# A language-model tower on one core: token gathers issued later in the front loop, factors one by one, beta by pairs behind the loop, and a re-ordered start of the attention loop

## The chip, the core and the metric

The kernel runs on one core of one Trainium2 chip. The metric is the device time of one execution in microseconds (us), the median of several runs. The core's engines work from queues of their own and meet at semaphores: TensorE (PE in the profile, its weight loads PEld), VectorE (DVE), ScalarE (ACT), GpSimd (POOL), and SyncE (SP), which here only issues DMAs.

## What is computed

Inputs are two rows of 1024 token ids. Three blocks follow one another, each added to the stream `h` of 2 x 1024 x 192 values:

```
tok = wte[ids];  Q = layernorm(tok)*gamma + beta, times W_proj.T;  V = tok @ W_val.T          (8 heads of 64)
traces = 0.99*(value_traces - erase(Q masked)/denom) + 0.1*(Q_masked^T V two tokens on)/denom
h  = (Q one token back @ traces) @ W_out.T
h += attention(layernorm(h)): softmax(q k^T * scale * (gw gw^T)), mixed with gw gw^T by sigmoid(alpha)
     gw = softmax(gelu(v @ W_gp))                                                  (49 groups)
h += soft mixture of 64 experts (layernorm(h)), dispatch and combine by softmax of x @ phi_n
```

`denom` is the count of masked tokens times 8, at least 1.

## The kernel before, in words

Tokens are worked in NT = 16 tiles of 128 (8 for each of the two rows of the batch, KT = 8). The order of every engine is written out by hand, as one program for each engine with waits on counting semaphores; an engine runs its program strictly in this order.

*Front loop.* The rows of `wte` come by NX = 18 indirect DMAs (`gather(g)`, L463), nine for each batch row, so that tile i of the first row is token block i, but tile i of the second row is block i + 1 (`tok_of`, L375: tile 8 is block 9, tile 15 is block 16). POOL issues them. Its program in the loop over i is: gather(i + 6), then `masked(i)` (L477, a masked copy of the normalised tile), then, for odd i, `front_factors(i + 2, i + 4)` (L471 and L472), which takes the statistics of two tiles and makes 1/sqrt(var) and -mean/sqrt(var). For these factors it waits until VectorE has done `stats` (L1534 to L1537) of both tiles, and `stats(i)` waits for block `tok_of(i)` to land.

Stage s of the front loop, on the other engines:
- ScalarE: the hi part of tile s - 2 (L1165), normalise tile s (L1157, waits for the factors), squares and masked copy of Q of tile s - 3 (L1172, L1177).
- TensorE: Q projection of tile s - 3 (`q_proj`, L597 to L601, waits for the lo part), two transposes of tile s - 1 (`tok_T`), two products with the next token block (`cprime(s - 2)`, L670 and L671, waits for `masked`), 16 small products (`grams(s - 5)`, L692).
- VectorE: the lo part of tile s - 2 (`lo_parts`, L1562 and L1563), norms and scaled Q of tile s - 4 (L1577 to L1587), then the statistics that `ahead(s)` lists: tiles 3 and 4 in stage 2, 5 in stage 3, 6 and 7 in stage 4, and tile s + 3 from stage 5 on.
- SyncE: weights of later stages, each load released by a count of `stats`: wT at 6, wvT and vt at 8, wpn at 10, woT, wpg and aw at 12.

Ahead of the loop TensorE makes the row beta x W_proj (L637, L638), the count of masked tokens (L642), and beta x W_proj once more with tokens' channels on the partitions (L645, L646), which VectorE copies to `bpair` (L1551).

*Behind the loop* the traces are mixed with W_out and the attention's q x k matrix is prepared in parts (`prepare`, SETUP); each part is rounded up on ScalarE and its remainder taken on VectorE (`round_off`, L1505; for the parts "B2" a further instruction, L1518, rewrites one row). Part "kB2" ends with the copy of `bpair` to `wpn`.

*Second loop* (16 tiles): mix, normalise, transpose, value projection (`value_proj`), and in its last four stages `query(0)` to `query(3)`; queries 4 and 5 and the transposes `gw_T(0)`, `gw_T(1)` of the group weights follow.

*Attention loop.* Stage s on TensorE: `scores(s)` (10 products into banks 0 and 1, 4 into banks 2 and 3), `turn(s - 1)` (8 transposes, L889), `attend(s - 1)` (L900, L901, 16 products L907). In stage 1, between scores and turn, stand `sums(0)` (L831), `gw_T(2)`, `gw_T(3)` and `sums(1)`, all waiting until VectorE has taken all eight queries; `turn(0)` then waits for both `u_take`. VectorE's stage: weight, copy of half of `et` (L1768), `z_tile(s)` (L1759), `finish(s - 1)`, and then `beside(s)`: the square sums of phi in stage 3 (L1733), its scaling in halves in stages 4 and 5 (L1739), the lo part of its first half in stage 7 (L1749) and of the rest in stage 8 (L1751). Dispatch, experts and combination follow.

## Time and profile before

| | us |
|---|---|
| median of 3 runs (463.87 to 464.69) | 464.32 |
| the profiled execution | 464.32 |
| its span in the trace | 462.5 |
| TensorE busy | 431.2 (93%) |
| VectorE busy | 297.3 (64%) |
| ScalarE busy | 228.5 (49%) |
| GpSimd busy | 145.4 (31%) |
| chain that ended last, TensorE's share | 69% |

```profile
PE   5889998999888999999999989999999889999995
DVE  6489873586765577676777676766965243443564
ACT  4577742588743446554232566877874312122220
POOL 5778600375010065120003490003540331212310
```

Each digit is the busy share, in tenths, of a slice of 11.6 us. The front loop fills slices 1 to 6, the second loop slices 8 to 10, the attention loop begins in slice 11. A row of a timeline reads: start, duration, engine, line, operation, output <- inputs, their sizes, and in brackets the engine's idle time just before and what ended it. A duration runs from an instruction's start to its end and can overlap its neighbours'; the distance of two starts is what an instruction costs its engine.

### The profile page before, as it was taken

What the parts mean: (1) busy time and instruction counts of PE and PEld (TensorE: products, weight loads), DVE (VectorE), ACT (ScalarE), POOL (GpSimd) and SP (SyncE); (2) the same over time, 40 slices, a digit from 0 to 9 for tenths busy, and PEclk for the clock granted to TensorE, in tenths of its full rate; (3) what the DMA queues carried; (4) which work ended last, traced back from release to release, by engine and by line L of the source; (5) the groups of instructions that cost most, each with busy time, mean ns of one, the idle gap of its engine ahead of it and who ended that gap; (6) DMA issues with size and microseconds to landing.
All of it is one profiled execution on the core that took longest, in us unless ns stands there. A gap on an engine that the chain in (4) does not pass through costs nothing.

```text
span 462.5 us, 8303 instructions
## 1 busy us (share of the span) xinstructions
PE 431.2 (93%) x3086; PEld 356.7 (77%) x3086; DVE 297.3 (64%) x776; ACT 228.5 (49%) x415; POOL 145.4 (31%) x235
## 2 busy tenths in 40 slices
PE   5889998999888999999999989999999889999995
PEld 2667755798777888988888878899975577787895
DVE  6489873586765577676777676766965243443564
ACT  4577742588743446554232566877874312122220
POOL 5778600375010065120003490003540331212310
PEclk9999999999999999999999999999999999999999
DMA  3343000200100000500000000003629999999404
GB/s 97 111 126 104 11 2 0 103 1 1 30 0 0 1 0 1 206 1 0 1 0 1 1 1 0 2 0 132 280 100 412 388 351 380 382 373 386 152 19 136
DMA packets 14231, 49.64 MB, mean 107 GB/s; under 512 B 3504, under 2 KB 8528, under 8 KB 9968
## 3 DMA queue, kind: packets, MB, share of 16 engines
q1 hardware_dynamic: 7584, 43.21, 24.8%
q0 software_dynamic: 2912, 3.37, 2.6%
q10 hardware_dynamic: 3696, 2.54, 1.8%
q8 instruction: 25, 0.41, 0.4%
q14 instruction: 14, 0.11, 0.1%
HBM read 45.94 MB, written 3.15 MB: 106 GB/s over the span
## 4 chain that ended last, share of the span: by engine, by line
PE 69%; DMA 12%; DVE 11%; POOL 3%; issue 2%; ACT 2%; SPq 0%; POOLq 0%; ACTq 0%; DVEq 0%
DMA w1r<-in_p_w 10%; PE ps L907 9%; PE ps L953 8%; PE ps L1110 6%; PE ps L1051 3%; PE ps L889 3%; PE ps L1080 2%; PE ps L933 2%; DMA tok<-in_L_tok_wte,ints 2%; PE ps L937 2%; PE ps L936 2%; PE ps L934 2%; PE ps L935 2%; PE ps L1097 2%; PE ps L854 1%
## 5 line engine op out<-in xcount | busy, mean ns | idle before, releaser
L907 PE MATMUL ps<-pr,et 128*128 128x192 f32 x256 | 46.6, 333 | 2.1 <-DVE et L1768 1.6
L1110 PE MATMUL ps<-ys,ct 128*128 128x192 f32 x256 | 45.2, 331 | 1.7 <-DMA ys<-ys_dram 1.7
L1937 DVE TENSOR_TENSOR res<-ps,res 128x384 f32<-128x384 f32 x64 | 35.7, 558 | 15.2 <-PE ps L1110 10.7
L907 PEld LDWEIGHTS ps<-pr,et 128*128 128x128 f32 x256 | 41.1, 189 | 5.4 <-ACT et L1332 3.1
L1110 PEld LDWEIGHTS ps<-ys,ct 128*128 128x128 f32 x256 | 41.2, 190 | 5.1 <-issue 4.8
L501 POOL TENSOR_SCALAR ve<-mv 128x1 f32<-128x1 f32 x32 | 12.1, 378 | 94.8 <-DVE mv L1783 54.0
L585 POOL DMA_DIRECT2D ys<-ys_dram x32 | 19.6, 617 | 69.8 <-DMA ys_dram<-ysb 68.7
L1451 ACT ACTIVATE hs<-ps 128x384 f32<-128x384 f32 x16 | 7.8, 490 | 58.5 <-PE ps L1051 58.5
L1321 ACT ACTIVATE scs<-ps,pr 128x1024 f32<-128x1024 f32 x16 | 17.8, 1115 | 29.2 <-PE ps L858 29.2
L1325 ACT ACTIVATE zz<-zz,nmx 128x1024 f32<-128x1024 f32 x16 | 18.4, 1150 | 27.7 <-DVE nmx L1762 27.4
L1928 DVE COPY ysb<-ps 128x192 f32<-128x192 f32 x16 | 5.7, 356 | 39.0 <-PE ps L1080 39.0
L1798 DVE CUSTOM_DVE_ANT_0 ec<-ps,zero 128x1024 f32<-128x1024 f32 x16 | 19.5, 1222 | 13.8 <-PE ps L937 13.8
L1051 PE MATMUL ps<-w1r,xsT 128*32 128x384 f32 x256 | 24.0, 492 | 1.7 <-DMA w1r<-in_p_w 1.6
L1457 ACT COPY ct<-ps 128x1024 f32<-128x1024 f32 x16 | 16.1, 1009 | 14.8 <-PE ps L1097 14.8
L953 PE MATMUL ps<-x2a,lsr 128*128 128x193 f32 x128 | 22.6, 327 | 0.0
L953 PE MATMUL ps<-x2b,lsr 128*128 128x193 f32 x128 | 21.7, 328 | 0.7 <-ACT lsr L1363 0.7
L502 POOL TENSOR_TENSOR rstd<-ve,mhalf 128x1 f32<-128x1 f32 x32 | 21.3, 667 | 2.7
L1768 DVE COPY et<-ps 128x512 f32<-128x512 f32 x16 | 11.1, 692 | 16.6 <-PE ps L889 16.5
L953 PEld LDWEIGHTS ps<-x2b,lsr 128*128 128x128 f32 x128 | 20.9, 190 | 1.0 <-ACT lsr L1363 1.0
L538 POOL TENSOR_TENSOR xve<-xve,mhalf 128x2 f32<-128x2 f32 x8 | 7.4, 921 | 45.2 <-DVE xve L1869 45.2
L953 PEld LDWEIGHTS ps<-x2a,lsr 128*128 128x128 f32 x128 | 20.8, 190 | 0.2
L463 POOL DMA_INDIRECT tok<-in_L_tok_wte,ints x18 | 18.5, 1025 | 7.8 <-issue 5.1
(318 smaller groups left out, 1197.6 us busy)
## 6 DMA issues: line engine op xcount, KB each, us to landing
w1r<-in_p_w SPq DMA_DIRECT2D x16, 1152.0 KB, 19.4
w2r<-in_p_w SPq DMA_DIRECT2D x16, 1152.0 KB, 19.2
ys_dram<-ysb ACTq DMA_DIRECT2D x16, 96.0 KB, 8.3
ys<-ys_dram POOLq DMA_DIRECT2D x32, 48.0 KB, 7.2
phT<-in_p_phi SPq DMA_DIRECT2D x1, 1024.0 KB, 4.6
wT<-in_p_qkv SPq DMA_DIRECT2D x1, 774.0 KB, 4.2
out<-res SPq DMA_DIRECT2D x3, 192.0 KB, 3.3
out<-res ACTq DMA_DIRECT2D x3, 192.0 KB, 3.8
```

Source lines behind the costliest of these rows:

```text
L463: nc.gpsimd.indirect_dma_start(tok[:, g, :], None, a["L0_tok_wte"], bass.IndirectOffsetOnAxis(ap=ints[:, g:g + 1], axis=0)).then_inc(gathe ...
L502: return nc.gpsimd.tensor_tensor(rstd[:, i:i + 1], ve[:, i:i + 1], mhalf[:, 0:1], ALU.pow)
L585: nc.gpsimd.dma_start(ys[rows, t % YR, b, :], y4[b]).then_inc(ys_loaded[t % YR], 16)
L907: last = mm(d[:, 0:D], et[:, k, :], pr[:, b * KT + k, 1:1 + D], start=(k == 0), stop=(k == KT - 1))
L953: last = mm(d, ls(b, k)[:, t * P:(t + 1) * P], x2(i)[:, 0:1 + D], start=(k == 0 and t % 2 == 0), stop=(k == KT - 1), skip_group_check=True)
L1051: last = mm(bank(0)[32 * j:32 * j + 32, 0:HID], xsT[:, half, GE * g + j, :, :].rearrange("d b s -> d (b s)"), w1r[r][:, 3 * (j // 2) + j % ...
L1110: last = mm(bank(5 + q % 3)[:, h * D:(h + 1) * D], ct[:, u % 2, k + h, :], ys[:, t % YR, b, :], start=True, stop=True)
L1321: sc.activation(scs[:], bank(0, 2), ACT.Identity, bias=pr[:, i, 0:1]).then_inc(m["s_copied"], 1)
L1325: sc.activation(zz[:, i % 2, :], zz[:, i % 2, :], ACT.Exp, bias=nmx[:, i:i + 1], accum_out=rsum[:, i:i + 1]).then_inc(m["e_ready"], 1)
L1457: sc.copy(ct[:, u % 2].rearrange("p k c -> p (k c)"), bank(3, 2)).then_inc(m["cT_copied"], 1)
L1798: v.tensor_tensor_reduce(ec(i), bank(logit_bank(i), 2), bc(zero[:], [P, NS]), 1.0, LOWEST, ALU.add, ALU.max, mxC[:, i:i + 1]).then_inc(m[" ...
L1937: v.tensor_tensor(res[:, i:i + 2, :], bank(5 + q % 3)[:, 0:2 * D].rearrange("p (h d) -> p h d", h=2), res[:, i:i + 2, :], ALU.add).then_in ...
```

## The change

- POOL: factors of tiles 1 and 2 are made one by one, tile 1's ahead of gather 3; gathers 5 and 6 no longer stand behind `masked(0)`; in the loop gather(i + 4) takes the place of gather(i + 6).
- VectorE: the statistics of tiles 1 and 2 stand ahead of the wait for beta; `ahead` becomes tiles 3 and 4 in stage 2, then 5, 6, 7 in stages 3 to 5, 8 and 9 in stage 6, tile s + 3 from stage 7 on. The count of masked tokens is taken in stage 2.
- TensorE: nine products of a tile of ones ahead of the wait for inputs; `cprime` one stage later; the products L645 and L646 go. In their place four products of one row with ones stand ahead of part "kB2", and `bpair` goes. L1518 goes from all "B2" parts.
- Second loop: only queries 0 and 1 stand in it; ScalarE takes them one stage earlier.
- Attention loop: `sums(0)` in stage 1 and `sums(1)` in stage 2, each waiting only for what it needs, `gw_T(2)` and `gw_T(3)` at the ends of stages 2 and 3, with their takes on ScalarE and VectorE; `z_tile(1)` ahead of `u_take(0)`; `norm_groups(1)` moves from stage 0 to the end of stage 1. Square sums of phi in stage 5, both halves of its scaling in stage 6, both lo parts in stage 8.

```diff
@@ POOL
+            front_factors(1, 2)
             gather(3)
+            front_factors(2, 3)
             gather(4)
-            front_factors(1, 3)
             pool.wait_ge(m["mask_ready"], 1)
             masked(0)
-            gather(5)
-            gather(6)
             for i in range(1, NT):
-                if i + 6 < NX:
-                    gather(i + 6)
+                if i + 4 < NX:
+                    gather(i + 4)
                 masked(i)
                 if i % 2 and i + 2 < NT:
                     front_factors(i + 2, min(i + 4, NT))
@@ PE
+            pe.wait_ge(m["ones_ready"], 1)
+            for k in range(9):
+                mm(bank(2)[:, 0:P], ones[:], ones[:], start=True, stop=True)
...
-            mm(bank(3)[:, 0:1], ones[:], msum[:], start=True, stop=True)
-            for t in range(HP):
-                c, o = slice(t * P, (t + 1) * P), slice(2 + 2 * t, 4 + 2 * t)
-                mm(bank(3)[:, o], wpT[:, 0, c], betA, start=True, stop=False)
-                last = mm(bank(3)[:, o], wpT[0:DB, 1, c], betB, start=False, stop=True)
-            last.then_inc(m["cnt_filled"], 1)
+            mm(bank(6)[:, 0:1], ones[:], msum[:], start=True, stop=True).then_inc(m["cnt_filled"], 1)
...
-                if 2 <= s < NT + 2:
-                    cprime(s - 2)
+                if 3 <= s < NT + 2:
+                    cprime(s - 3)
+                if s == NT + 1:
+                    cprime(NT - 1)
...
+            for t in range(HP):
+                mm(setup_bank("kB2")[:, 272 + 2 * t:274 + 2 * t], wpT[DB:DB + 1, 1, t * P:(t + 1) * P],
+                   ones[DB:DB + 1, 0:2], start=True, stop=True)
             prepare("kB2", at["kA"] + 1)
...
-                if s > NT:
+                if NT < s <= NT + 2:
                     query(s - NT - 1)
...
             def sums(b):
 
-                pe.wait_ge(m["qpl_taken"], 2 * QPS)
+                pe.wait_ge(m["gw_ready"], b + 1)
+                pe.wait_ge(m["qpl_taken"], 2 * QPS - 2 + b)
...
-                if s == 1:
-                    sums(0)
-                    for j in range(GTS, NB * GTS):
-                        gw_T(j)
-                    sums(1)
+                if 1 <= s <= NB:
+                    sums(s - 1)
                 if s >= 1:
                     turn(s - 1)
...
+                if 2 <= s < 2 + GTS:
+                    gw_T(s)
@@ DVE
-                    link(remainder(B2[DB:DB + 2, :], d[DB:DB + 2, 0:n], scale[2], B2[DB:DB + 2, :]))
-                    last = v.tensor_scalar(B2[DB:DB + 1, :], d[DB:DB + 1, 0:n], scale[3], None, ALU.mult)
+                    last = remainder(B2[DB:DB + 1, :], d[DB:DB + 1, 0:n], scale[2], B2[DB:DB + 1, :])
...
-                if s <= 4:
-                    return {2: [3, 4], 3: [5], 4: [6, 7]}.get(s, [])
+                if s <= 6:
+                    return {2: [3, 4], 3: [5], 4: [6], 5: [7], 6: [8, 9]}.get(s, [])
                 return [s + 3] if s + 3 < NT else []
...
             for s in range(NT + 1):
                 if s == 1:
-                    u_take(0)
-                    for j in range(GTS, NB * GTS):
-                        gw_lo(j)
-                    u_take(1)
+                    z_tile(1)
+                if 3 <= s < 3 + GTS:
+                    gw_lo(s - 1)
+                if 1 <= s <= NB:
+                    u_take(s - 1)
```

## Rows read from the trace of the kernel before

**Rows 1.** The page, busy time by engine: share of span, instructions
```profile
PE 431.2 (93%) x3086; PEld 356.7 (77%) x3086; DVE 297.3 (64%) x776; ACT 228.5 (49%) x415; POOL 145.4 (31%) x235
```

**Rows 2.** DVE timeline, front loop: start, us, line, form, idle before
```profile
31.30 0.36 DVE L1534 BATCH_NORM_STATS2 st<-tok 128x6 f32<-128x192 f32 x1 [0.58 <-DMA tok<-in_L_tok_wte,ints]
...
32.05 0.28 DVE L1562 TENSOR_TENSOR XL<-ps,XH 128x128 fp32r<-128x128 f32 x1
...
35.11 0.28 DVE L1562 TENSOR_TENSOR XL<-ps,XH 128x128 fp32r<-128x128 f32 x1
...
37.26 0.35 DVE L1534 BATCH_NORM_STATS2 st<-tok 128x6 f32<-128x192 f32 x1
...
49.82 0.28 DVE L1562 TENSOR_TENSOR XL<-ps,XH 128x128 fp32r<-128x128 f32 x1
```

**Rows 3.** POOL timeline, front loop
```profile
8.57 0.28 POOL L472 TENSOR_TENSOR nmr<-nmean,rstd 128x1 f32<-128x1 f32 x1
...
17.69 0.79 POOL L477 TENSOR_SCALAR xm<-xh,mask 128x192 f32<-128x192 f32 x1
...
18.43 0.73 POOL L471 TENSOR_TENSOR rstd<-ve,mhalf 128x2 f32<-128x2 f32 x1
...
24.98 0.72 POOL L471 TENSOR_TENSOR rstd<-ve,mhalf 128x2 f32<-128x2 f32 x1 [1.11 <-DVE ve L1537]
...
26.52 1.07 POOL L463 DMA_INDIRECT tok<-in_L_tok_wte,ints  x1 [0.48 <-issue]
...
30.37 0.74 POOL L471 TENSOR_TENSOR rstd<-ve,mhalf 128x2 f32<-128x2 f32 x1
...
31.93 1.05 POOL L463 DMA_INDIRECT tok<-in_L_tok_wte,ints  x1 [0.48 <-issue]
```

**Rows 4.** DMA issues at 26 to 27, and at 33.5 to 34.5
```profile
tok<-in_L_tok_wte,ints POOLq DMA_INDIRECT x1, 4.8
...
tok<-in_L_tok_wte,ints POOLq DMA_INDIRECT x1, 2.7
```

**Rows 5.** SP timeline, 0 to 60
```profile
25.66 0.33 SPq L403 DMA_DIRECT2D wvT<-in_p_wv  x1
```

**Rows 6.** PE timeline, front loop, early and later
```profile
16.71 0.63 PE L599 MATMUL ps<-wpAh,XL 128*128 128x512 f32 x1
...
26.64 0.39 PE L599 MATMUL ps<-wpAh,XL 128*128 128x512 f32 x1
```

**Rows 7.** PE timeline, 68 to 97
```profile
71.12 0.49 PE L716 MATMUL ps<-bs,wvT 128*128 128x128 f32 x2
```

**Rows 8.** DVE timeline, 56 to 84
```profile
79.35 0.42 DVE L1518 TENSOR_SCALAR kvB<-ps 1x257 fp32r<-1x257 f32 x1
```

**Rows 9.** PE timeline, from the second loop into the attention loop
```profile
114.77 0.40 PE L790 MATMUL ps<-X1H,kvAh 128*128 128x512 f32 x1
...
115.93 0.28 PE L597 MATMUL ps<-kvAh,X1H 128*128 128x242 f32 x1
...
121.44 1.09 PE L822 MATMUL ps<-ident,gw 128*128 128x128 f32 x8 [1.30 <-DVE gw L1658]
...
132.82 2.87 PE L831 MATMUL ps<-pr,gw 128*128 128x192 f32 x16 [1.57 <-DVE qB L1688]
...
141.14 1.07 PE L889 MATMUL ps<-ident,zz 128*128 128x128 f32 x8 [1.97 <-DVE uP L1725]
...
171.66 2.97 PE L907 MATMUL ps<-pr,et 128*128 128x192 f32 x16
```

**Rows 10.** DVE timeline, attention loop
```profile
172.32 0.69 DVE L1768 COPY et<-ps 128x512 f32<-128x512 f32 x1
```

**Rows 11.** DVE timeline, later in the attention loop
```profile
190.37 1.19 DVE L1749 TENSOR_TENSOR ph<-phT,ph 128x1024 fp32r<-128x1024 f32 x1
...
199.52 0.27 DVE L1793 TENSOR_TENSOR X2L<-ps,X2H 64x128 fp32r<-64x128 f32 x1
```

**Rows 12.** PE timeline, later in the attention loop
```profile
199.94 1.07 PE L889 MATMUL ps<-ident,zz 128*128 128x128 f32 x8
```

More of the change, by code:

```diff
@@ L184, in build @@
         eyeP = sb("eyeP", [P, DT], where=front)
-        bpair = sb("bpair", [P, 2 * HP], where=front)
         r1 = sb("r1", [P, HP, DT], where=front)
@@ L817, in gw_T @@
                 if b:
-                    pe.wait_ge(m["qpl_taken"], 2 * QPS)
+                    pe.wait_ge(m["et_copied_v"] if r else m["et_copied_a"], 2 + r)
                 else:
@@ L832, in sums @@
                 last.then_inc(m["u_filled"], 1)
-            for j in range(QPS, QPS + 2):
+            for j in range(2, QPS + 2):
                 query(j)
@@ L898, in attend @@
                     pe.wait_ge(m["o_taken"], i - 1)
+                else:
+                    pe.wait_ge(m["u_taken"], i + 1)
                 d = bank(6 + i % 2)
@@ L1379, in _ @@
             for s in range(NT + 1):
+                if 3 <= s < 3 + GTS:
+                    gw_hi(s - 1)
                 if s < NT:
@@ L1611, in _ @@
                     stats(i)
+                if s == 2:
+                    count()
                 if s == KT + 2:
@@ L1710, in behind_first_scores @@
             def behind_first_scores():
-                norm_groups(1)
                 for j in range(QPS + 2, 2 * QPS):
@@ L1734, in beside @@
                                     ).then_inc(m["ph_summed"], 1)
[L1735 to L1742 removed]
+                if s == 6:
+                    dve.wait_ge(m["ph_rsqrt"], 1)
+                    for h in range(2):
+                        w = phT[:, h, :].rearrange("d (n p) -> d n p", p=NP)
+                        last = v.tensor_tensor(w, w, bc(prs[:, h, :].unsqueeze(1), [P, NE, NP]), ALU.mult)
+                    last.then_inc(m["ph_scaled"], 1)
+                if s == 7:
                     dve.wait_ge(m["in_phi"], 16 * 4)
@@ L1823, in _ @@
                 if s == 1:
-                    u_take(0)
-                    for j in range(GTS, NB * GTS):
-                        gw_lo(j)
-                    u_take(1)
+                    z_tile(1)
+                if 3 <= s < 3 + GTS:
+                    gw_lo(s - 1)
+                if 1 <= s <= NB:
+                    u_take(s - 1)
                 if s >= 1:
@@ L1833, in _ @@
                     x2_lo(KT + 1)
-                if s < NT:
+                if s < NT and s != 1:
                     z_tile(s)
@@ L1839, in _ @@
                     finish(s - 1)
+                if s == 1:
+                    norm_groups(1)
                 beside(s)
```

67 lines of the change are left out of this document (28 added, 39 removed).

## The prediction

> **What bounds the kernel now.** I read the page's busy times first: TensorE is busy for 431.2 us of 462.5 [rows 1], so on the whole TensorE sets the time, and only its idle time can be won or lost. That is an average. I then read, stage by stage, which wait ends last, in the timelines of the single engines.
>
> In the front loop VectorE sets the pace and TensorE just keeps up. From the lo part of tile 6 at 35.11 to the next statistics at 37.26 VectorE needs 2.15 us (lo part, norms, scaled Q), and 0.75 us for the statistics of one tile (31.30 to 32.05). The lo part of tile 5 stands at 32.05 and that of tile 11 at 49.82, six stages in 17.8 us, and the only idle time of note ahead of them is 0.58 us for token block 10 [rows 2]. POOL is ahead: its gathers land two stages before VectorE wants them. A microsecond lost by VectorE here moves everything behind, since each later stage takes the front loop's result.
>
> In the start of the attention loop TensorE stands idle three times: 1.30 us for the group weights, 1.57 us for the last queries' lo parts, 1.97 us for `u_take` [rows 9]. From then on it is full.
>
> **The change, part by part: the gathers.** POOL works in order. Its factors end at 8.85 (8.57 + 0.28) for tile 0. Behind that now stand two single factor pairs (a double one takes 1.56 - 0.48 = 1.08 us, from 30.37 to the next gather at 31.93 less the 0.48 ahead of it; I take 1.0), gathers 3 to 5 (1.07 each and some 0.13 between, 3.6 together) and two masked copies (0.79 each, 1.6). Factors (3, 5) start at 8.85 + 2.0 + 3.6 + 1.6 = 16.1 instead of 18.43, since two gathers went from ahead of them: 2.3 us won. From there to factors (5, 7) the way over ScalarE and VectorE is the same, 24.98 - 18.43 = 6.55 us, so they come at 22.7 [rows 3].
>
> From here the later issue costs. Tile 8 is token block 9. Factors (7, 9) wait in POOL's iteration 5 for the statistics of tile 8, and gather 9 is now issued in that same iteration, two stages later than before. It starts at 22.7 + 1.56 (factors and gap) + 1.07 (gather 8) + 0.8 + 0.17 (masked copy and gap) = 26.3. Before, a gather issued at 26.52 landed after 4.8 us, an undisturbed one after 2.7 [rows 3, 4]; the first went out 0.86 us behind the load of wvT, at 25.66 [rows 5]. That load hangs on the statistics of tile 7; these now end at some 25.3 to 25.6, so gather 9 meets it again, and I take 4.8. Block 9 lands at 31.1, the statistics of tile 8 end at 31.85.
>
> VectorE's next instruction in the same stage 6 is the statistics of tile 9, block 10, and gather 10 is queued on POOL behind the factors that waited for tile 8. So VectorE stops with nothing else to do: 0.06 us of signal, 1.56 (factors and gap), 2.7 (landing), together 4.32 us, then 0.75. The lo part of tile 5, queued behind this on VectorE, with TensorE waiting for it, comes at 31.85 + 4.32 + 0.75 = 36.9 instead of 32.05: 4.9 us late. Had gather 9 landed in 2.7, it would be 2.8.
>
> The same ring holds in stages 8, 10 and 12: statistics of stage s - 1, factors, gather s + 4, statistics of stage s. It takes 4.32 us; VectorE has 2.15 us of other work in it, so it stands for 2.17 us each time. In the odd stages the gather follows a masked copy only (issued 1.07 + 0.8 + 0.17 = 2.04 us after the previous one, landing 4.74 us after it) while VectorE needs 2.7 + 0.75 + 2.15 = 5.6 from that gather, so nothing waits. Three stalls are 6.5 us. Front loop: 4.9 + 6.5 = **11.4 us lost**. Bounds: 9.3 with gather 9 undisturbed; 4 us more if each of two further gathers meets a weight load as gather 10 did (2.1 each), so 15.5.
>
> **The first microseconds.** The products of ones run while nothing else could. Their form is not in the trace; the nearest pair on 128 columns lasts 0.49 us, some 0.42 of it from start to start, and in the start a product takes 0.63 us that takes 0.39 later [rows 6, 7]. Nine end between 1.3 + 9 x 0.42 = 5.1 and twice that length, 8.9; inputs land at 5.4. Beta's row is wanted by ScalarE ahead of the first tile. I take zero: between nothing, and 2 us either way, as the first factors at 8.85 hold the first tile anyhow. `cprime` one stage later removes TensorE's waits for the masked copy, but TensorE waits for VectorE now.
>
> About the clock: the stretch's granted clock reads 1.00 throughout, yet 0.63 against 0.39 us for one form says that TensorE started at the 1.2 GHz level and later had 2.4 [rows 6]. The Trainium skill, page "TensorE: Matmul & The Clock Gate", section "Part 1: The HAM clock gate", says that an array left idle goes back to 1.2 GHz. No stall of TensorE in the front loop of before is long enough to show that. The stall in stage 6 will be far longer, and by that rule the sum would grow; this is a rival below.
>
> **Behind the loop.** Four products of one row each, as pairs: 4 x 0.42 = 1.7 us at the form of L716 (shorter rows may halve that), on the path to "kB2" [rows 7]. L1518 goes from "kB2" and "vB2", 0.42 us each, both on the path [rows 8]. Sum +0.8 at most, -0.8 if the products hide; I take **+0.4**. The `bpair` copy stays as a copy from PSUM.
>
> **Attention.** Value projection of tile 15 stood behind query 2, from 114.77 to 115.93; it now comes 1.16 us earlier, and with it GELU, exp and the group weights that TensorE waits for (1.30 idle): 1.16 won. `sums(0)` waits only for bank 6, free by then: 1.57 won. `gw_T` and `sums(1)` leave the way to `turn(0)`: 1.97 won [rows 9]. New waits take their place: attend(0) for `u_take(0)` (0.9 us of VectorE behind `sums(0)`, 0.8 of it under `turn(0)`), the same in stage 2, and `sums(1)` for `norm_groups(1)`; together 0.7. So 4.0 won.
> Against it: the second half of phi's scaling moves to stage 6, behind the wait for the first. There the copy of `et` ended at 173.01 (172.32 + 0.69), and TensorE, in attend from 171.66, wanted it at its half, 1.3 us in [rows 9, 10]. No slack, so the 1.19 us of one such pass [rows 11] is paid in full. In stage 8 the first lo pass (1.19) joins the second; the lo part of x2 ended at 199.79 and released the transposes at 199.94 [rows 11, 12]: again no slack, 1.19 paid. Attention: -4.0 + 2.4 = **-1.6**, between -4.0 (both passes covered) and -0.5.
>
> **Sum**, against the profiled execution, 464.32, which is also the median (span 462.5 and 1.8 outside it): 464.3 + 11.4 + 0.4 - 1.6 = **474.5 us**.
>
> **Rivals.**
> 1. *TensorE falls to 1.2 GHz in the stall of stage 6 and is slow for a while.* A stage costs it 2.85 us at full clock, 5.7 at half, against 3.99 us that the ring leaves per stage (7.97 per pair). Two slow stages cost 3.4 us: 477.9; slow until stage 12, six stages, would be 484.6. For: it was slow in the start; against: VectorE's ring gives it room. Chance 0.18.
> 2. *Gather 9 misses the load* (landing 2.7 us) and attention keeps its 4.0: 474.5 - 2.1 - 2.4 = 470.0. Chance 0.15.
> 3. *Faster than before.* The gathers still land in time, since VectorE reaches their statistics later than I place it: then the 2.3 us won at the start stay, and 464.3 - 2.3 + 0.4 - 1.6 = 460.8. It decides at stage 6: gather 10 would have to start 2.7 us before VectorE is through with tile 8. Against it stands POOL's order itself. Chance 0.05.
> 4. *The change doesn't do what it says* at the gathers (POOL issues ahead of its waits): the front loop as before, 463. Chance 0.02.
> The forecast keeps 0.60, between 472 and 477.
>
> **How the numbers follow.** The range takes in rival 2 and the first form of rival 1 with their spread: 468.5 to 480.5; below it lie rivals 3 and 4, above it a clock that stays low. Some 0.2% (0.9 us) is what a measurement can tell from no change. Faster by more: 0.06; within: 0.02; slower: 0.92.
>
> **What would show it.** In the trace of the changed kernel: factors (3, 5) near 16; gather 9 near 26; in stage 6 VectorE idle twice ahead of its statistics, the second time for over 4 us; then some 2.2 us idle ahead of the statistics of tiles 11, 13 and 15; the lo part of tile 11 near 61. TensorE's 512-column products behind the long stall at 0.39 or 0.63 us decide rival 1. Idle times ahead of `gw_T(0)`, `sums(0)` and `turn(0)` under 0.4 us; stages 6 and 8 of the attention loop longer by 1.2. Wrong if the stalls for token blocks are missing, or if tile 8's block were already there.

## The result and the profile after

The kernel with the change takes 475.93 us, median of four runs (474.74 to 477.03), beside 464.35 us for the kernel before on the same chip. By these medians it is 11.6 us slower. The ratio of the two kernels, 1.0228 with a 95% interval of 1.0195 to 1.0261, is an estimate of its own and not the quotient of the two medians (1.0249, inside the interval); it says 10.6 us. The profiled execution took 474.74 us, with a span of 472.9 us. Single executions of three kernels below (482.65 us of a_fill_stalls, 472.04 of a_lead5, 493.56 of gp_one_by_one) ran in a slower state of the chip and don't enter the ratios.

The page's head: span, busy time by engine, then TensorE's busy tenths and granted clock in 40 slices.

```profile
span 472.9 us, 8321 instructions
PE 438.6 (93%) x3096; PEld 362.0 (77%) x3096; DVE 296.0 (63%) x771; ACT 228.5 (48%) x415; POOL 146.6 (31%) x237
PE   7957799999999999989999989999999889999995
PEclk9697899999999999999999999999999999999999
```

TensorE is 7.4 us longer busy than in [rows 1], and the span is 10.4 us longer. The share of busy time did not move; the largest difference stands in the first eight slices, where TensorE shows gaps and a lower clock.

GpSimd's timeline of the front loop (start, duration, line, form, idle before; L470 and L471 are the factors, L462 a gather):

```profile
16.33 0.74 POOL L470 TENSOR_TENSOR rstd<-ve,mhalf 128x2 f32<-128x2 f32 x1
23.47 0.73 POOL L470 TENSOR_TENSOR rstd<-ve,mhalf 128x2 f32<-128x2 f32 x1 [1.69 <-DVE ve L1539]
27.09 1.00 POOL L462 DMA_INDIRECT tok<-in_L_tok_wte,ints  x1 [0.17 <-issue]
31.73 0.72 POOL L470 TENSOR_TENSOR rstd<-ve,mhalf 128x2 f32<-128x2 f32 x1 [2.81 <-DVE ve L1539]
33.27 1.08 POOL L462 DMA_INDIRECT tok<-in_L_tok_wte,ints  x1 [0.48 <-issue]
```

VectorE's timeline of the same stretch (L1536 statistics, L1565 lo part):

```profile
30.81 0.36 DVE L1536 BATCH_NORM_STATS2 st<-tok 128x6 f32<-128x192 f32 x1 [1.60 <-DMA tok<-in_L_tok_wte,ints]
36.03 0.36 DVE L1536 BATCH_NORM_STATS2 st<-tok 128x6 f32<-128x192 f32 x1 [4.39 <-DMA tok<-in_L_tok_wte,ints]
36.77 0.28 DVE L1565 TENSOR_TENSOR XL<-ps,XH 128x128 fp32r<-128x128 f32 x1
...
44.11 0.36 DVE L1536 BATCH_NORM_STATS2 st<-tok 128x6 f32<-128x192 f32 x1 [2.23 <-DMA tok<-in_L_tok_wte,ints]
...
52.22 0.36 DVE L1536 BATCH_NORM_STATS2 st<-tok 128x6 f32<-128x192 f32 x1 [2.26 <-DMA tok<-in_L_tok_wte,ints]
...
60.61 0.36 DVE L1536 BATCH_NORM_STATS2 st<-tok 128x6 f32<-128x192 f32 x1 [2.26 <-DMA tok<-in_L_tok_wte,ints]
61.36 0.28 DVE L1565 TENSOR_TENSOR XL<-ps,XH 128x128 fp32r<-128x128 f32 x1
```

Read the two together. The statistics of tile 8 (30.81) release the factors at 31.73, behind which gather 10 is queued (33.27); VectorE's next instruction needs exactly that block and stands 4.39 us. Then the ring repeats three times at 2.2 us. The answering rows of before are [rows 2] (0.58 us of idle time, once) and [rows 3].

TensorE, at places that stand in both kernels. Of after: behind the long wait, the first product of the preparation behind the loop, the weights' products (L745), the transposes of tile 13 in the second loop (the last but two), the group weights' transposes, `turn(8)`, and the dispatch products (L957) behind the last wait for `lsr`:

```profile
37.30 0.80 PE L595 MATMUL ps<-wpAh,XH 128*128 128x512 f32 x1 [7.03 <-DVE XL L1566]
...
38.74 0.63 PE L598 MATMUL ps<-wpB,XH 128*128 128x512 f32 x1
...
80.59 0.70 PE L614 MATMUL ps<-wT 128*128 128x257 f32 x2
...
92.14 5.77 PE L745 MATMUL ps<-mm,wpn 128*66 128x192 f32 x24 [1.16 <-issue]
...
122.49 0.30 PE L764 MATMUL ps<-ident,x1t 128*128 128x128 f32 x1 [0.93 <-DVE X1L L1679]
...
133.62 1.09 PE L822 MATMUL ps<-ident,gw 128*128 128x128 f32 x8
...
210.88 1.07 PE L891 MATMUL ps<-ident,zz 128*128 128x128 f32 x8 [1.22 <-DVE X2L L1795]
...
346.49 4.84 PE L957 MATMUL ps<-x2b,lsr 128*128 128x193 f32 x28 [0.73 <-ACT lsr L1367]
```

And of before, the same places that its rows above did not show:

```profile
69.03 0.70 PE L616 MATMUL ps<-wT 128*128 128x257 f32 x2
...
80.06 4.09 PE L745 MATMUL ps<-mm,wpn 128*66 128x192 f32 x24 [1.62 <-issue]
...
93.20 0.30 PE L764 MATMUL ps<-ident,x1t 128*128 128x128 f32 x1 [0.45 <-DVE X1L L1674]
...
109.17 0.30 PE L764 MATMUL ps<-ident,x1t 128*128 128x128 f32 x1 [0.94 <-DVE X1L L1674]
...
335.54 4.84 PE L953 MATMUL ps<-x2b,lsr 128*128 128x193 f32 x28 [0.74 <-ACT lsr L1363]
```

So the front loop ends 11.56 us later (80.59 against 69.03). The stretch up to L745 adds 0.52 (92.14 - 80.59 against 80.06 - 69.03), L745 itself 1.68, 5.77 instead of 4.09 us for the same 24 products, and the wait of 0.45 us for X1L at 93.20 is gone: 13.32 us at the transposes of tile 13 (122.49 against 109.17). From there to these dispatch products the new kernel takes 224.00 us instead of 226.37, so the attention part gives 2.37 us back. That leaves 10.95 us at the dispatch products, and 10.4 at the end, since the wait for `ys` further on is 1.1 instead of 1.7 us.

These two places, `T` (transposes of tile 13) and `X` (the dispatch products), carry the comparison of all kernels. A name that begins with a_ starts from the new kernel, one with b_ from the kernel before, ag_ from a_gathers_as_before, gp_ from ag_phi_pairs:

| kernel | T, us | X, us | X - T | L745's products | median, us |
|---|---|---|---|---|---|
| before | 109.17 | 335.54 | 226.37 | 4.09 | 464.35 |
| after | 122.49 | 346.49 | 224.00 | 5.77 | 475.93 |
| a_gathers_as_before | 109.03 | 333.09 | 224.06 | 4.09 | 462.35 |
| b_late_gathers | 124.08 | 350.54 | 226.46 | 5.77 | 479.57 |
| a_late_pairs | 121.66 | 345.73 | 224.07 | 4.09 | 473.03 |
| ag_phi_spread | 108.42 | 330.32 | 221.90 | 4.09 | 460.47 |
| b_attention | 109.24 | 333.34 | 224.10 | 4.09 | 462.77 |
| a_fill_stalls | 120.97 | 344.96 | 223.99 | 4.09 | 475.35 |
| a_lead5 | 112.39 | 336.45 | 224.06 | 4.09 | 465.23 |
| ag_phi_pairs | 108.62 | 330.41 | 221.79 | 4.09 | 459.06 |
| b_front | 110.81 | 337.25 | 226.44 | 5.77 | 465.71 |
| gp_no_ones | 108.19 | 329.99 | 221.80 | 4.09 | 458.60 |
| gp_one_by_one | 108.81 | 331.34 | 222.53 | 4.09 | 459.60 |
| gp_factors_first | 107.71 | 329.56 | 221.85 | 4.09 | 457.55 |

T and X come from one profiled execution each. Unlike the medians they are free of what happens behind X, where waits for expert weights and for `ys` differ by 1 to 2 us between the profiles (1.7 us for `ys` in before, 1.1 in the new kernel, 3.4 in a_fill_stalls). But T has a spread too: a_gathers_as_before, ag_phi_spread and ag_phi_pairs have the same program up to the preparation behind the front loop, and its first product starts at 68.80, 68.19 and 69.25 us. So 1.1 us of T can be chance without any fall of the clock. The medians come from four groups of runs, in which the kernel before took 464.35 (the first two rows), 465.35, 464.93 and 465.82 us; between groups the ratios are the fairer comparison.

### The profile page after: what moved, and what is told of

Its sections match the earlier page's. It is cut to its first block, busy times and chain, and to the rows that moved or that the text cites. A ratio compares the mean times of both kernels' runs of the same rounds, so it can differ in the third digit from the quotient of the medians.

```text
span 472.9 us, 8321 instructions
## 1 busy us (share of the span) xinstructions
PE 438.6 (93%) x3096; PEld 362.0 (77%) x3096; DVE 296.0 (63%) x771; ACT 228.5 (48%) x415; POOL 146.6 (31%) x237
## 4 chain that ended last, share of the span: by engine, by line
PE 65%; DMA 14%; DVE 11%; POOL 5%; issue 3%; ACT 1%; SPq 0%; POOLq 0%
PE ps L911 8%; PE ps L957 8%; PE ps L1113 7%; DMA w1r<-in_p_w 5%; DMA tok<-in_L_tok_wte,ints 5%; PE ps L1054 3%; PE ps L891 2%; PE ps L1100 2%; PE ps L937 2%; DMA ys<-ys_dram 2%; PE ps L1083 2%; DMA ys_dram<-ysb 2%; PE ps L941 2%; PE ps L939 2%; PE ps L938 2%
## 5 line engine op out<-in xcount | busy, mean ns | idle before, releaser
L911 PE MATMUL ps<-pr,et 128*128 128x192 f32 x256 | 46.6, 332 | 3.0 <-DVE et L1770 2.5
L911 PEld LDWEIGHTS ps<-pr,et 128*128 128x128 f32 x256 | 41.1, 189 | 6.1 <-DVE et L1770 3.4
L499 POOL TENSOR_SCALAR ve<-mv 128x1 f32<-128x1 f32 x32 | 10.9, 339 | 84.6 <-DVE mv L1785 41.6
L1329 ACT ACTIVATE zz<-zz,nmx 128x1024 f32<-128x1024 f32 x16 | 18.4, 1151 | 25.6 <-DVE nmx L1764 25.4
L1460 ACT COPY ct<-ps 128x1024 f32<-128x1024 f32 x16 | 16.1, 1009 | 14.8 <-PE ps L1100 14.8
L957 PE MATMUL ps<-x2a,lsr 128*128 128x193 f32 x128 | 22.6, 327 | 0.0
L957 PE MATMUL ps<-x2b,lsr 128*128 128x193 f32 x128 | 21.7, 327 | 0.7 <-ACT lsr L1367 0.7
L957 PEld LDWEIGHTS ps<-x2b,lsr 128*128 128x128 f32 x128 | 20.9, 190 | 1.0 <-ACT lsr L1367 1.0
L462 POOL DMA_INDIRECT tok<-in_L_tok_wte,ints x18 | 18.6, 1035 | 7.7 <-issue 4.9
L957 PEld LDWEIGHTS ps<-x2a,lsr 128*128 128x128 f32 x128 | 20.8, 190 | 0.2
L1761 DVE CUSTOM_DVE_ANT_0 zz<-scs,ps 128x1024 f32<-128x1024 f32 x16 | 19.4, 1211 | 1.7 <-PE ps L876 1.2
```

Of the source, the lines that this page charges most:

```text
L462: nc.gpsimd.indirect_dma_start(tok[:, g, :], None, a["L0_tok_wte"], bass.IndirectOffsetOnAxis(ap=ints[:, g:g + 1], axis=0)).then_inc(gathe ...
L911: last = mm(d[:, 0:D], et[:, k, :], pr[:, b * KT + k, 1:1 + D], start=(k == 0), stop=(k == KT - 1))
L957: last = mm(d, ls(b, k)[:, t * P:(t + 1) * P], x2(i)[:, 0:1 + D], start=(k == 0 and t % 2 == 0), stop=(k == KT - 1), skip_group_check=True)
L1329: sc.activation(zz[:, i % 2, :], zz[:, i % 2, :], ACT.Exp, bias=nmx[:, i:i + 1], accum_out=rsum[:, i:i + 1]).then_inc(m["e_ready"], 1)
L1761: v.tensor_tensor_reduce(zz[:, i % 2, :], scs[:], bank(2, 2), 1.0, LOWEST, ALU.mult, ALU.max, zmx[:, i:i + 1]).then_inc(m["z_ready"], 1)
```

## The experiments

### The gathers, undone and done alone

a_gathers_as_before is the new kernel with GpSimd's order and VectorE's table of statistics of before:

```diff
             front_factors(0, 1)
-            front_factors(1, 2)
             gather(3)
-            front_factors(2, 3)
             gather(4)
+            front_factors(1, 3)
...
             masked(0)
+            gather(5)
+            gather(6)
             for i in range(1, NT):
-                if i + 4 < NX:
-                    gather(i + 4)
+                if i + 6 < NX:
+                    gather(i + 6)
```

> The changed kernel with POOL's program (factors, gather lead of six) and the order of statistics as before; all else of the change stays. Theory (the ring of gather, statistics and factors costs some 11.5 us): the front loop ends near 69 to 70 again and the time is near 462.5 us, a little under the kernel before, since the attention part wins 2.8 and the hand-over costs some 1 to 2. Rival (the gathers are only a part of it, the rest is the clock and the products of ones at the start): 466 or more, with the first products of the loop still slow after TensorE's idle time near 8 to 10.

Measured: 462.35 us, ratio 0.9941 (0.9917 to 0.9965). T falls back from 122.49 to 109.03. Without its gathers the change gains some 2.7 us by the ratio; with them it loses 11.6. So the whole loss comes with this one part, 13 to 14 us (13.46 by T, of which 1.68 are L745's products). The part has three pieces, the lead of the gathers, the first factors one by one and the table of statistics; the next two experiments separate them in part.

b_late_gathers is the kernel before with the late gathers and their table of statistics alone:

```diff
             masked(0)
-            gather(5)
-            gather(6)
             for i in range(1, NT):
-                if i + 6 < NX:
-                    gather(i + 6)
+                if i + 4 < NX:
+                    gather(i + 4)
...
-                if s <= 4:
-                    return {2: [3, 4], 3: [5], 4: [6, 7]}.get(s, [])
+                if s <= 6:
+                    return {2: [3, 4], 3: [5], 4: [6], 5: [7], 6: [8, 9]}.get(s, [])
```

> The kernel before with one thing changed: gathers four blocks ahead instead of six (gathers 5 and 6 no longer behind the first masked copy) and the new order of statistics. Theory: the ring alone gives the loss, one stall of over 4 us in stage 6 and three of 2.2 us, so 473.5 to 476.5 us. Rival (part of the loss comes from TensorE's part of the change): under 470.

Measured: 479.57 us, ratio 1.0328 (1.0286 to 1.0370), more than expected. VectorE's waits are those of the new kernel:

```profile
30.96 0.36 DVE L1532 BATCH_NORM_STATS2 st<-tok 128x6 f32<-128x192 f32 x1 [2.06 <-DMA tok<-in_L_tok_wte,ints]
36.20 0.36 DVE L1532 BATCH_NORM_STATS2 st<-tok 128x6 f32<-128x192 f32 x1 [4.42 <-DMA tok<-in_L_tok_wte,ints]
44.24 0.36 DVE L1532 BATCH_NORM_STATS2 st<-tok 128x6 f32<-128x192 f32 x1 [2.18 <-DMA tok<-in_L_tok_wte,ints]
```

By the profile the excess is the clock's. T stands 14.91 us behind before, and two stretches at and behind the end of the ring ran partly at the lower clock. One window of each (from, to, us; then the engines' busy time; last the granted clock, the DMA share and GB/s):

```profile
65.00:70.00 5.00, 5.00 (x47) 4.02 (x47) 2.94 (x8) 2.86 (x7) 1.85 (x3) 0.84 0.02 3
...
95.00:100.00 5.00, 4.04 (x19) 3.74 (x17) 1.67 (x4) 1.78 (x4) 0.00 (x0) 0.76 0.00 0
```

From 60 to 70 us (0.82 and 0.84) that is 5 x 0.18 + 5 x 0.16 = 1.7 us of missing clock, in L745 another 1.68; 14.91 less both is 11.5, the ring's price. The expectation held no clock term at all. The first of the two follows the last wait of the ring, 2.32 us, behind which no further wait for a gather can hide it (TensorE's timeline; the form of L669 takes 0.49 us at the full clock):

```profile
61.98 0.50 PE L595 MATMUL ps<-wpAh,XH 128*128 128x512 f32 x1 [2.32 <-DVE XL L1561]
...
64.33 0.85 PE L669 MATMUL ps<-tok,xm 128*65 128x192 f32 x2
...
82.20 0.70 PE L614 MATMUL ps<-wT 128*128 128x257 f32 x2
```

The preparation starts at 82.20 and not at 80.59 as in the new kernel, so this fall was paid, and it is the prediction's first rival at work: TensorE slow behind a wait of the ring. That the median lies as far above before, 14.2 us, suggests that other runs paid such falls too; only the profiled one shows them.

### One gather more ahead

a_lead5 is the new kernel with gathers five blocks ahead instead of four:

```diff
             masked(0)
+            gather(5)
             for i in range(1, NT):
-                if i + 4 < NX:
-                    gather(i + 4)
+                if i + 5 < NX:
+                    gather(i + 5)
```

> The kernel after with one gather more ahead: gather 5 behind masked(0), then gather i+5 instead of i+4 in each step; VectorE's table of statistics stays. Theory 1 (the lead of the gathers sets the stalls, one place is about 2 us): gather 9 goes out near 25.2 instead of 27.09, VectorE's wait ahead of tile 9 falls from 4.39 to 2.5 and those ahead of tiles 11, 13, 15 from 2.2 to at most 0.4, so some 7.5 of the 11.6 us of the front loop come back: 468 (466.5 to 469.5). Rival (gather 9 now flies beside the 0.5 MB load and lands later): 4.39 stays, only the three of 2.2 go: 469.5 to 471. Another: both leads are far from what is needed, each wait shrinks by under 1 us: above 472.

Measured: 465.23 us, ratio 0.9998 (0.9977 to 1.0019). One place is worth 10.7 us by the medians and by the ratios alike: more than any reading expected. Table and first factors are those of the new kernel, so the lead alone carries most of the loss. GpSimd's and VectorE's rows show why:

```profile
25.21 1.06 POOL L462 DMA_INDIRECT tok<-in_L_tok_wte,ints  x1 [0.48 <-issue]
...
27.28 1.01 POOL L462 DMA_INDIRECT tok<-in_L_tok_wte,ints  x1 [0.17 <-issue]
...
30.32 0.72 POOL L470 TENSOR_TENSOR rstd<-ve,mhalf 128x2 f32<-128x2 f32 x1 [1.21 <-DVE ve L1540]
...
31.86 1.07 POOL L462 DMA_INDIRECT tok<-in_L_tok_wte,ints  x1 [0.48 <-issue]
```

```profile
31.33 0.36 DVE L1537 BATCH_NORM_STATS2 st<-tok 128x6 f32<-128x192 f32 x1 [1.09 <-DMA tok<-in_L_tok_wte,ints]
...
36.24 0.36 DVE L1537 BATCH_NORM_STATS2 st<-tok 128x6 f32<-128x192 f32 x1 [1.83 <-DMA tok<-in_L_tok_wte,ints]
```

Gather 10 now goes out at 27.28, ahead of the factors that wait for tile 8 (30.32), and not behind them. It is 6.0 us earlier than the 33.27 of the new kernel, though it moved by one place in the program. My expectation priced a place at the 2 us between neighbouring gathers; what counts is which side of a waiting instruction the place is on. T comes 10.10 us sooner: 8.4 us of the front loop (L745 starts at 83.70 instead of 92.14) and the 1.68 of its clock, which may be chance. Some 3 us are left against a lead of six (T 112.39 against 109.03): gather 11 still stands behind the factors, and the row at 36.24, tile 10, waits 1.83 us for it.

### The clock in the waits

The prediction's first rival asked whether TensorE's own slow stretch behind the long wait costs anything. a_fill_stalls gives it products to do there, whose results are thrown away:

```diff
+            FILL = {5: 13, 9: 4, 11: 1}
...
+                if i in FILL:
+                    pe.wait_ge(m["qw_ready"], i - 2)
+                    for n in range(FILL[i]):
+                        mm(q_bank(i)[:, 0:P], ones[:], ones[:], start=True, stop=True)
                 pe.wait_ge(m["xl_ready"], i + 1)
```

> The kernel after with products of ones (thrown away) in TensorE's three longest waits of the front loop: 13 ahead of the query product of tile 5 (wait 7.03), 4 ahead of tile 9 (2.59), 1 ahead of tile 11. They take at most 6.1, 1.9 and 0.5 us at the full clock, so they end before the wait does. Theory 1 (the gathers' chain over GpSimd and VectorE sets the loop's pace, the clock's fall in 35 to 42 us is hidden behind it): stage times stay, lo part of tile 11 near 61, and the time is that of the kernel after, 474.5 to 476.5. Rival (TensorE at 1.2 GHz lengthens the path): the granted clock of 35 to 42 us and of 55 to 58 us is 1.00, the end of the front loop comes 2 to 3 us sooner, and the time is 472 to 474.

Measured: 475.35 us (474.19 to 482.65), ratio 1.0227 (1.0190 to 1.0265), as with a loop that the gathers pace. As a remedy it half failed: the 26 passes took only 3.17 us, and a wait of 4.31 us was left where 7.03 had been.

```profile
29.82 3.17 PE L675 MATMUL ps<-ones 128*128 128x128 f32 x26
...
37.30 0.79 PE L595 MATMUL ps<-wpAh,XH 128*128 128x512 f32 x1 [4.31 <-DVE XL L1571]
...
92.29 4.09 PE L750 MATMUL ps<-mm,wpn 128*66 128x192 f32 x24 [1.16 <-issue]
```

The clock fell there all the same (0.64 from 35 to 40 us). But from 55 to 60 us it read 1.00 instead of the new kernel's 0.69, and L750, the former L745, starts no earlier for it (92.29 against 92.14). So that fall was hidden in the ring. The one behind 37.30 remained in both and is not tried by itself; that it is hidden too is read from VectorE's rows, where the lo part of tile 6 follows 2.88 us behind that of tile 5, as at the full clock, and the next statistics wait 2.23 us for a DMA. T comes 1.52 us sooner, all from L750 at 4.09 us; behind X, a wait for `ys` of 3.40 us (1.1 in the new kernel) took most of it back, and the profiled execution is 0.55 us shorter.

a_late_pairs moves the four one-row products behind kB2, where TensorE waits for VectorE:

```diff
-            for t in range(HP):
-                mm(setup_bank("kB2")[:, 272 + 2 * t:274 + 2 * t], wpT[DB:DB + 1, 1, t * P:(t + 1) * P],
-                   ones[DB:DB + 1, 0:2], start=True, stop=True)
             prepare("kB2", at["kA"] + 1)
+            for t in range(HP):
+                last = mm(bank(4)[:, 2 * t:2 + 2 * t], wpT[DB:DB + 1, 1, t * P:(t + 1) * P],
+                          ones[DB:DB + 1, 0:2], start=True, stop=True)
+            last.then_inc(m["pairs_filled"], 1)
```

> The changed kernel with the four one-row products for beta issued behind part kB2 instead of ahead of it, into a bank of their own, so that they fill a wait. Theory 1 (the light products lower TensorE's clock for the 24 products of L745 behind them, and cost 1.0 us of their own): they still stand just ahead of L745, so the clock still falls and only the 1.0 us is won, 474.9 against 475.9. Theory 2 (it is the idle time behind kB2 that lowers the clock): with the wait filled, L745 lasts 4.1 instead of 5.8 us, and 2.7 us are won.

Measured: 473.03 us (470.88 to 474.38), ratio 1.0152 (1.0118 to 1.0186), 2.9 us below the new kernel by the medians, 3.5 by the ratios. The profile doesn't carry all of it: T is only 0.83 us sooner. L745 took 4.09 us again, but in this execution the clock fell from 60 to 70 us instead (0.76 and 0.90, 1.7 us missing), right behind the ring's last wait as in b_late_gathers, and the preparation starts late by as much:

```profile
82.25 0.70 PE L614 MATMUL ps<-wT 128*128 128x257 f32 x2
```

From there to the weights' products it is 10.69 us (92.94 less 82.25) against 11.55 in the new kernel, so the edit itself gives 0.86. The rest I put to falls that an execution has or hasn't; that is argued. Neither theory holds as a rule for L745: in a_gathers_as_before the one-row products stand ahead of it, with the same 1.16 us of idle time, and it takes 4.09 us. ag_phi_pairs repeats the same edit on a kernel whose profile had no such fall, ag_phi_spread (below):

> The kernel after with the gathers' order and the statistics' table of before, the phi steps spread over stages 4 to 8, and the four one-row products behind kB2, where TensorE waits. Against the kernel without this last edit (460.47): Theory 1, the one-row products (1.05 us) now lie in a wait of 1.16 and the stretch behind ran at the full clock already, so 0.8 us faster, 459.6. Rival, the 2.9 us that the same edit gave in the kernel after come again: 457.6. That would mean that the clock is not what they came from.

Measured: 459.06 us, ratio 0.9899 (0.9864 to 0.9935), beside 460.47 us for the kernel without the edit in another group of runs; but the ratios are 0.9899 and 0.9897, and T is no earlier (108.62 against 108.42). The trace says why: the preparation happened to start 1.06 us later (69.25 against 68.19), and from there to the weights' products it took 10.69 us instead of 11.56. So Theory 1 has its 0.8 us in the stretch that the edit touches, too little for the medians to tell; it is not 2.9 us again.

### The attention part alone, and phi's passes spread

b_attention is the kernel before with the change's parts from the second loop on alone. Its core:

```diff
-                if s > NT:
+                if NT < s <= NT + 2:
                     query(s - NT - 1)
...
-                if s == 1:
-                    sums(0)
-                    for j in range(GTS, NB * GTS):
-                        gw_T(j)
-                    sums(1)
+                if 1 <= s <= NB:
+                    sums(s - 1)
...
+                if 2 <= s < 2 + GTS:
+                    gw_T(s)
```

> The kernel before with the second-loop part alone: two queries instead of four, weights' transposes spread over three steps, sums over tokens one step apart, the second half's z tile and group norm moved, and the phi steps two stages later. Theory 1 (the prediction's working): TensorE wins 4.0 us at the head of attention, two phi scalings on VectorE cost 2.4 back, so 1.6 us faster, ratio 0.9966. Rival: by the landmarks of the kernel after (scores(0) to scores(4) gives back 3.4 us, turn(8) loses 2.2) together with what the one-byte order of queries gives ahead of scores(0) (1.6), the gain is 5.0 and the cost 2.2, so 2.8 us faster, ratio 0.994. A third: the part gains nothing alone since its waits only move (ratio 0.9995 to 1.0005).

Measured: 462.77 us (461.41 to 464.62), ratio 0.9956 (0.9937 to 0.9974), so 2.0 us faster, 1.2 to 2.9. X - T is 224.10 against 226.37 us: 2.27 won. Both sit between the two sums expected, 1.6 and 2.8.

ag_phi_spread is a_gathers_as_before with phi's passes spread over stages 4 to 8:

```diff
-                if s == 6:
-                    dve.wait_ge(m["ph_rsqrt"], 1)
-                    for h in range(2):
-                        w = phT[:, h, :].rearrange("d (n p) -> d n p", p=NP)
...
+                if s in (5, 6):
+                    if s == 5:
+                        dve.wait_ge(m["ph_rsqrt"], 1)
+                    w = phT[:, s - 5, :].rearrange("d (n p) -> d n p", p=NP)
...
```

and likewise the first lo pass in stage 7 instead of 8.

> The first of these kernels with phi's work spread again, one stage earlier than in the change: square sums in stage 4, the scaling in halves in stages 5 and 6, the two lo parts in stages 7 and 8. Theory (each doubled VectorE pass costs TensorE its 1.2 us): 2.2 us faster than the first, near 460.3. Rival (the waits come from something else in these stages): no change against the first.

Measured: 460.47 us, ratio 0.9897 (0.9874 to 0.9921); X - T is 221.90 instead of 224.06. Those 2.16 us are the price of phi's joined passes, and with it paid back TensorE's gain at the head of attention is 226.37 - 221.90 = 4.47 us. In the new kernel the joined scaling stands on VectorE as 2.36 us in one piece, and TensorE waits 0.99 us behind it (VectorE's timeline, then TensorE's); the joined lo parts cost it the 1.22 us of waiting at `turn(8)` that the row at 210.88 above shows:

```profile
193.79 2.36 DVE L1743 TENSOR_TENSOR phT<-phT,prs 128x1024 f32<-128x1024 f32 x2 [1.95 <-POOL prs L522]
```

```profile
197.26 1.57 PE L911 MATMUL ps<-pr,et 128*128 128x192 f32 x8 [0.99 <-DVE et L1770]
```

### The start

b_front is the kernel before with the rest of the change, gathers and statistics as before. Its core:

```diff
+            pe.wait_ge(m["ones_ready"], 1)
+            for k in range(9):
+                mm(bank(2)[:, 0:P], ones[:], ones[:], start=True, stop=True)
...
-            for t in range(HP):
-                c, o = slice(t * P, (t + 1) * P), slice(2 + 2 * t, 4 + 2 * t)
-                mm(bank(3)[:, o], wpT[:, 0, c], betA, start=True, stop=False)
...
+            for t in range(HP):
+                mm(setup_bank("kB2")[:, 272 + 2 * t:274 + 2 * t], wpT[DB:DB + 1, 1, t * P:(t + 1) * P],
```

> The kernel before with the first part alone and without its gathers: nine products of ones ahead of the inputs, the count product and the four one-row pairs moved, the beta row in one piece, tile 0's pair product one step later, the first loop's tables of gathers and statistics as before. Theory 1 (the prediction's working: ones at zero, one-row pairs +0.4 behind the loop) and the landmarks of the kernel with the gathers as before (109.03 against 109.17 us at the transposes of x1): within 0.5 us of the kernel before, ratio 0.999 to 1.001, although the granted clock stands at half from 10 to 20 us. Rival (that half clock is on the path): 1 to 2 us slower. Another (the shorter start wins): 1 to 2 us faster.

Measured: 465.71 us, ratio 1.0008 (0.9982 to 1.0033): no difference. But its profile has a fall of the clock in L745's products that a_gathers_as_before, with the same program up to there, lacks:

```profile
80.41 5.77 PE L746 MATMUL ps<-mm,wpn 128*66 128x192 f32 x24 [1.16 <-issue]
```

```profile
80.35 4.09 PE L746 MATMUL ps<-mm,wpn 128*66 128x192 f32 x24 [1.16 <-issue]
```

The first row is b_front's, the second a_gathers_as_before's: the same 24 products, 0.06 us apart, with the same 1.16 us of idle time ahead. What makes the clock fall in the one and not in the other stays open.

The last three start from ag_phi_pairs. gp_no_ones drops the nine products of ones:

```diff
-            for k in range(9):
-                mm(bank(2)[:, 0:P], ones[:], ones[:], start=True, stop=True)
```

gp_one_by_one takes the change's order for the first factors:

```diff
             front_factors(0, 1)
+            front_factors(1, 2)
             gather(3)
+            front_factors(2, 3)
             gather(4)
-            front_factors(1, 3)
```

gp_factors_first, on top of that, puts a factor pair ahead of two gathers:

```diff
             masked(0)
             gather(5)
+            masked(1)
+            front_factors(3, 5)
             gather(6)
-            for i in range(1, NT):
+            gather(7)
+            for i in range(2, NT):
```

> The fastest kernel so far (459.06) without the nine products of ones at its start. Theory 1 (they lie in a wait and what follows is bound by the gathers and the factors): no change, 458.6 to 459.6, and the granted clock of the first 10 us reads the same or lower. Rival (they keep the clock up for the beta products that release the first query product): beta products last 3.1 us instead of 2.4 and the time is 1 us higher.

Measured: 458.60 us (457.97 to 462.36), ratio 0.9874 (0.9829 to 0.9920); T 108.19 against 108.62. Without the products of ones the two beta products last 1.87 and 1.86 us instead of 1.38 and 1.02. They do keep the clock up there, as the rival said, but nobody waits for it: no change in the time.

> The fastest kernel so far (459.06) with GpSimd's first factors one by one (tile 1 alone, gather 3, tile 2 alone, gather 4), all gathers at the lead of before. Theory 1: TensorE's second transposes come 1.8 us sooner (wait of 2.81 falls to 1), but factors (3,5) stay near 18 behind gathers 5 to 7, and the wait of 3.65 on VectorE grows instead: 459, no change. Rival: every later stage moves up: 457.5 to 458.

Measured: 459.60 us, ratio 0.9866 (0.9826 to 0.9906), T 108.81: no change. The wait moved to VectorE, 4.18 us ahead of tile 2 (21.63) instead of 3.65.

> The kernel of the run before this one (factors one by one) with factors (3,5) ahead of gathers 6 and 7 on GpSimd: they start near 15.3 instead of 17.75. Theory 1 (the chain of factors and gathers sets the pace of the first six stages): VectorE's wait of 3.65 ahead of tile 2 falls to about 1.2, tiles 3 to 5 move up by 1.5 to 2.4, and the kernel ends at 457 (456.5 to 457.7). Rival (tile 9's row is late anyway, its wait of 1.11 grows by what is won): 459, no change.

Measured: 457.55 us (457.23 to 458.20), ratio 0.9831 (0.9799 to 0.9862), the lowest median of all, 18.4 us below the new kernel's. VectorE's wait ahead of tile 2 fell from 4.18 to 1.64 us:

```profile
19.70 0.29 DVE L1572 TENSOR_TENSOR XL<-ps,XH 128x128 fp32r<-128x128 f32 x1 [1.64 <-ACT XH L1174]
```

T comes 1.1 us sooner than in gp_one_by_one, about half of the 2 expected. The factors start at 16.35, not at 15.3 as I had put them; of the 1.9 us won at tile 2 (19.70 against 21.63) 1.1 are left at the preparation. That is about the spread of 1.06 us named above, and another 0.7 us of the difference between the two profiled executions lies between T and X, where their programs are equal. The two ratios' intervals overlap; for a gain speak the executions of one group, 457.23 to 458.20 against 458.79 to 459.79 (493.56 aside). So that it is faster is likely, and how much of it is the order's doing is not shown. Both lie clearly below a_gathers_as_before, which has phi's joined passes still.

## Why the prediction was right

**The ring of gathers.** The forecast of 11.4 us for the front loop met 11.56, and its steps hold one by one. Factors (3, 5) at 16.33 (16.1 said); the long wait 4.39 us (4.32); the lo part of tile 5 at 36.77 (36.9); three further waits of 2.23, 2.26 and 2.26 (2.17 each); the lo part of tile 11 at 61.36 (near 61). Two small errors cancelled each other: factors (5, 7) came at 23.47 and gather 9 at 27.09, 0.8 us later than worked out, but its block was read at 30.81, 3.7 us later and not 4.8. The rest of the front loop, from the lo part of tile 11 on, ran as before (the preparation 19.23 us behind it, 19.21 in before). a_gathers_as_before and a_lead5 show the mechanism by taking it away.

**The start.** Taken as 2.3 us won at the factors and then lost in the ring, and zero for the products of ones. b_late_gathers, with before's paired factors, comes to tile 8 at 30.96 against 30.81, so the one-by-one order carries nothing into the ring. b_front (ratio 1.0008) and gp_no_ones confirm the zeros.

**Behind the loop.** The term was +0.4; from the preparation's first product to L745 it was 11.55 us (92.14 less 80.59) against 11.03 (80.06 less 69.03), +0.5. The four one-row pairs took 1.05 us, not 1.7.

**The clock, the missing term.** Rival 1 had the right event; in the new kernel's profile it cost nothing where it was expected. TensorE fell to 1.2 GHz behind the long wait: granted clock 0.50 from 35 to 40 us and 0.89 in the five behind, 0.63 us for the products of 512 columns from 37.88 to 39.16 and 0.39 again from 42.24. By VectorE's rows this was hidden in the ring, as the rival's own "against" had it. In b_late_gathers and a_late_pairs a fall behind the ring's last wait was not hidden and cost 1.6 to 1.7 us, so the rival is real, at one slow stage and not two. What was paid is a fall that nobody priced, 1.68 us in L745's products, some 50 us further on, with 1.16 us of idle time ahead of them (1.62 in before, where it did not fall). The Trainium skill, page "TensorE: Matmul & The Clock Gate", section "Part 1: The HAM clock gate", says that an idle array goes back to 1.2 GHz, and of the change upwards that its moment varies from run to run. The fall behind the wait of 7.03 us agrees with the first. That a fall, too, comes in one execution and not in another is what the pair b_front and a_gathers_as_before shows: equal work up to there, 5.77 and 4.09 us.

**Attention.** -1.6 was forecast; -2.37 was measured in the trace, -2.0 by b_attention's ratio. The idle times of 1.30, 1.57 and 1.97 us at its head are gone from TensorE's rows. The two halves of the term were a little too small and too large: TensorE's gain 4.47 us (4.0 said), phi's joined passes 2.16 us (2.4 said). The 0.7 us set aside for new waits at `attend(0)` and `sums(1)` are not in the trace as waits: the first two groups of L911 (147.32 and 157.53) and `sums(1)` (153.39) have none. So the size of this term was the prediction's weakest step beside the clock.

**The sum.** 464.3 + 11.4 + 0.4 - 1.6 = 474.5. By the trace: 11.56 + 0.52 + 1.68 (clock) - 0.44 (X1L) - 2.37 - 0.5 (`ys` and the like) = 10.4, and the profiled execution took 474.74 us. So the forecast of the ring was right by its mechanism, and that the sum came within 0.3 us of this execution has luck in it: the unpriced fall of the clock (+1.68) and the smaller unpriced gains (-0.44, -0.5, and 0.8 of attention) cancelled. The median, 475.93, lies 1.2 us above that execution and 1.4 above the forecast, about one fall of the clock more; that it is one is argued and not shown, since only one execution has a trace.

## What to carry to other kernels

On a queue that works in order, a prefetch is worth what stands between it and its reader: a gather moved by one place came 6.0 us sooner, since it passed an instruction that waits for the reader's own engine. Before a prefetch is made later, follow the ring (statistics, factors, gather, statistics) and put its length against the work that the waiting engine has inside it; here 4.3 against 2.15 us. And a step that is ready early should stand ahead of prefetches that aren't urgent, not behind them: gp_factors_first against gp_one_by_one, 1.9 us at tile 2 in the trace and 2.0 in the median, though what of it reaches the end is not shown apart from chance.

## What the runs showed of the hardware

**The clock's fall is not a property of the kernel alone.** In kernels with equal instructions up to 80 us, the same 24 products ran in 4.09 and in 5.77 us. In four of fourteen profiles (after, b_late_gathers, a_late_pairs, b_front) a fall was paid there or from 60 to 70 us, in ten neither. Each such fall costs some 1.7 us, and b_late_gathers paid two. The falls from 60 to 70 us stand only in kernels with the late gathers, behind the ring's last wait of 2.3 us, in two of four such kernels (b_late_gathers and a_late_pairs, not after and a_fill_stalls); the fall in the 24 products came with and without late gathers. Places before and behind these stretches have to be compared.

**The granted clock reads 1.00 where the engine is slow, early on.** In the kernel before the products of 512 columns take 0.63 us up to the one at 16.71 us [rows 6] and 0.39 from the one at 17.44 on. Yet its windows (columns as above) say:

```profile
10.00:20.00 10.00, 9.53 (x37) 8.13 (x38) 5.30 (x27) 3.40 (x10) 7.37 (x12) 1.00 0.28 74
```

In the new kernel, where the products of ones had brought the clock up before 7.04 us and it fell again, the same stretch reads:

```profile
10.00:20.00 10.00, 8.18 (x23) 5.66 (x23) 4.99 (x26) 4.94 (x13) 8.40 (x14) 0.52 0.20 50
```

There the product takes 0.63 us from 12.83 to 18.86 and 0.41 at 21.04. So before was slow in this window for some 7.3 us too, which its record doesn't show: an estimate from the durations is 3.6 us of missing clock, beside the 4.8 that the new kernel's record shows. Most of these 4.8 us, out of the 11.8 that the mean clock (0.973 against 0.998) suggests as lost, are no difference. The Trainium skill, page "TensorE: Matmul & The Clock Gate", section "Part 1: The HAM clock gate", warns that clock events in a trace can be unreliable; here the durations decide.

**Products of ones do bring the clock up, for nothing.** Beta's two products took 1.86 us each in before, 1.84 and 1.02 in the new kernel, 1.38 and 1.02 in ag_phi_pairs. TensorE then waited twice for the first tiles (1.50 and 0.98 us in the new kernel) and was back at the slow level for the first products that count: 0.80 us for L595 at 12.24, which later takes 0.50, and 0.63 for the next, at 12.83.

**A gather beside a weight load** (gather 9 at 27.09, with the load of wvT issued at 26.30) took 3.7 us from its issue to its reader here, against 4.8 to landing in [rows 4] and 2.8 for gather 10 at 33.27, when no load was in flight.
